# Cross-attention on one core: two max-row transfers a slot instead of four, and `wo` loaded ahead of slot 0

## The reference, cut to what matters

```python
Q = (query @ w_q.T).reshape(B, S, 16, 32).transpose(0, 2, 1, 3)
K = (key @ w_k.T).reshape(B, -1, 16, 32).transpose(0, 2, 1, 3)
V = (value @ w_v.T).reshape(B, -1, 16, 32).transpose(0, 2, 1, 3)
scores = jnp.einsum('bhqd,bhkd->bhqk', Q, K) / np.sqrt(32)
attn = jax.nn.softmax(scores, axis=-1)
ctx = jnp.einsum('bhqk,bhkd->bhqd', attn, V).transpose(0, 2, 1, 3).reshape(B, S, 512)
x = ctx @ w_o.T + b_o + query
mu = jnp.mean(x, axis=-1, keepdims=True)
var = jnp.mean(jnp.square(x - mu), axis=-1, keepdims=True)
return (x - mu) * jax.lax.rsqrt(var + 1e-5) * ln_gamma + ln_beta
```

## Time and profile before

| | |
|---|---|
| median of 3 executions | 559.01 us (558.89 to 560.57) |
| profiled execution, its time | 557.26 us |
| its span | 555.5 us |
| TensorE (PE) matmul busy | 532.4 us, 96% |
| VectorE (DVE) busy | 465.2 us, 84% |
| GpSimd (POOL) busy | 424.2 us, 76% |
| ScalarE (ACT) busy | 393.6 us, 71% |

### The profile page before, as it was taken

One profiled execution on the slowest core, in us unless ns is written; L12 is line 12 of the kernel. 1 busy time (PEld: TensorE's weight loads), 2 busy tenths in 40 slices (PEclk: granted clock), 3 DMA queues, 4 the chain that ended last, 5 costly groups with the idle time before them and its releaser, 6 DMA issues.

```text
span 555.5 us, 12699 instructions
## 1 busy us (share of the span) xinstructions
PE 532.4 (96%) x4522; PEld 363.1 (65%) x4522; DVE 465.2 (84%) x874; ACT 393.6 (71%) x733; POOL 424.2 (76%) x391
## 2 busy tenths in 40 slices
PE   8988899999999999999999999999999999998991
PEld 6755566766676666666676667666676667665561
DVE  7877668888888888988889888988888888988785
ACT  7636767777777777777777777777777777766662
POOL 1714678888888888888888888888888888776665
PEclk9999999999999999999999999999999999999997
DMA  8434552443344334443343334343343432222122
GB/s 312 143 86 122 153 167 70 131 130 95 95 131 131 102 93 125 131 122 88 110 133 108 112 105 127 107 128 100 118 114 106 133 102 84 86 67 69 48 76 95
DMA packets 74111, 63.23 MB, mean 114 GB/s; under 512 B 46528, under 2 KB 46528, under 8 KB 74048
## 3 DMA queue, kind: packets, MB, share of 16 engines
q1 hardware_dynamic: 74048, 62.42, 37.0%
HBM read 39.58 MB, written 16.78 MB: 101 GB/s over the span
## 4 chain that ended last, share of the span: by engine, by line
PE 84%; DVE 5%; SPq 3%; DMA 3%; POOL 2%; issue 2%; ACT 1%; POOLq 0%; DVEq 0%; ACTq 0%
PE ps_q L410 45%; PE ps_o L416 12%; PE ps_c L372 10%; PE ps_s L345 7%; PE ps_s L355 3%; PE ps_q L283 2%; PE ps_s L283 2%; PE ps_o L283 2%; SPq L217 2%; DMA wo_raw<-in_woT 2%; DMA max_rows<-max_turned 1%; DVE half_max L703 1%; POOL y L879 1%; PE ps_c L290 1%; POOL y L877 1%
## 5 line engine op out<-in xcount | busy, mean ns | idle before, releaser
L410 PE MATMUL ps_q<-x_hi,wq_lo 64*128 64x512 f32 x448 | 185.8, 415 | 1.2 <-DVE values L668 1.1
L416 PE MATMUL ps_o<-wo_hi,c_lo 64*128 64x512 f32 x448 | 186.3, 416 | 0.0
L416 PE MATMUL ps_o<-wo_hi,c_hi 64*128 64x512 f32 x448 | 175.4, 392 | 0.0
L410 PE MATMUL ps_q<-x_hi,wq_hi 64*128 64x512 f32 x448 | 175.3, 391 | 0.0
L410 PE MATMUL ps_q<-x_lo,wq_hi 64*128 64x512 f32 x448 | 175.1, 391 | 0.0
L416 PE MATMUL ps_o<-wo_lo,c_hi 64*128 64x512 f32 x448 | 174.7, 390 | 0.0
L410 PEld LDWEIGHTS ps_q<-x_hi,wq_lo 64*128 64x128 f32 x448 | 82.5, 184 | 74.6 <-DVE z L747 44.4
L877 POOL TENSOR_TENSOR y<-y,gamma_row 128x512 f32<-128x512 f32 x60 | 77.8, 1296 | 58.4 <-ACT y L562 58.4
L849 POOL TENSOR_TENSOR x_lo<-xT_raw,x_hi 128x512 fp32r<-128x512 f32 x60 | 77.4, 1290 | 27.3 <-ACT x_hi L497 23.3
L855 POOL TENSOR_TENSOR c_lo<-c_raw,c_hi 128x512 fp32r<-128x512 f32 x64 | 82.9, 1295 | 16.7 <-ACT c_hi L497 16.7
L410 PEld LDWEIGHTS ps_q<-x_hi,wq_hi 64*128 64x128 f32 x448 | 82.6, 184 | 16.2
(11 more groups left out here) (104 smaller groups left out, 1113.6 us busy)
## 6 DMA issues: line engine op xcount, KB each, us to landing
xT_raw<-in_xT SPq DMA_DIRECT2D x64, 256.0 KB, 3.2
x_raw<-in_x SPq DMA_DIRECT2D x64, 256.0 KB, 2.8
out<-y SPq DMA_DIRECT2D x64, 256.0 KB, 2.4
max_rows<-max_turned SPq DMA_DIRECT2D x256, 16.0 KB
ctx_raw<-in_ctxT SPq DMA_DIRECT2D x4, 256.0 KB, 4.7
wk_raw<-in_wkT SPq DMA_DIRECT2D x4, 256.0 KB, 4.8
wq_raw<-in_wqT SPq DMA_DIRECT2D x4, 256.0 KB, 5.8
wv_raw<-in_wvT SPq DMA_DIRECT2D x4, 256.0 KB, 6.6
```

The costliest lines, as they stand in the source:

```text
L410: return nc.tensor.matmul(ps_q[:, 0, :], w[l][half, k, dims], x_[r][half, qc % 2, k, :], start=(half is lower and k == 0 and step == 0), s ...
L416: return nc.tensor.matmul(ps_o[:, 0, :], cx[l][half, k, tile], wo[r][half, k, :], start=(half is upper and k == 0 and step == 0), stop=(ha ...
```

## The change

It does five things.

1. The low part of the maxima is no longer a third part of `max_hl` but is written into quadrants 1 and 3 of part 1, with two reductions of 32 partitions in place of one of 128. `max_turned` has 32 columns instead of 64, and `fill_max_rows` issues two transfers instead of four. The rows of `select` follow.
2. `wo` is loaded in four transfers, one for each quadrant of 32 partitions and all four slices. They are issued before slot 0, and behind them the bias row, gamma, beta and tiles 0 to 3 of x. Tiles 4 to 7 of x stay in slots 2 to 5, one in each.
3. In slots 1 to 3 `subtract_max(t - 1)` stands before `project_values`.
4. In slot 6 VectorE does `odd_values` before `turn_max`; for slot 61 it does `turn_max` before `divide` and `statistics`.
5. At the end ScalarE makes the shift of tiles 59, 60 and 61 itself, in two small activations, `invert_deviation(57)` moves ahead of `context_to_hi(62)`, and VectorE does `finish(58)` before `statistics(59)`.

```diff
-        max_hl, max_turned = sb("max_hl", [P, 3, 32], fp32r), sb("max_turned", [P, 2, 32], fp32)
+        max_hl, max_turned = sb("max_hl", [P, 2, 32], fp32r), sb("max_turned", [P, 32], fp32)
...
-                        row = 64 * pair + 8 * part + 4 * head + pair
+                        row = 64 * pair + 4 * head + 2 * part + pair
...
-                for pair in range(2):
-                    for part in range(2):
-                        row = 64 * pair + 8 * part
-                        sp.dma_start(max_rows[row:row + 8, n % 2, :].bitcast(fp32).rearrange("p (b j) -> p b j", j=32),
-                                     max_turned[:, part, :]).then_inc(max_rows_filled[n % 2], 16)
+                for row in (0, 64):
+                    sp.dma_start(max_rows[row:row + 8, n % 2, :].bitcast(fp32).rearrange("p (b j) -> p b j", j=32),
+                                 max_turned[:, :]).then_inc(max_rows_filled[n % 2], 16)
...
+            for quadrant, head in enumerate((0, 2, 1, 3)):
+                sp.dma_start(wo_raw[DK * quadrant:DK * (quadrant + 1), :, :],
+                             woT.rearrange("(k h d) n -> h d k n", k=KT, h=4)[head, :, :, :]).then_inc(wo_loaded, 16)
+            sp.dma_start(bias_row[:, :], b_o.partition_broadcast(P)).then_inc(bias_loaded, 16)
+            for row, src in ((gamma_row, gamma), (beta_row, beta)):
+                sp.dma_start(row[:, :], src.partition_broadcast(P)).then_inc(gains_loaded, 16)
+            for i in range(4):
+                load_x(i)
+            sp.wait_ge(keys_zeroed, 2)
+            sp.wait_ge(keys_lo_done, G)
             for t in range(OUT_LAG):
                 fill_max_rows(t)
                 load_ahead(t)
-
-                if 1 <= t <= KT:
-
-                    for head in range(2):
-                        sp.dma_start(wo_raw[64 * head:64 * (head + 1), t - 1, :],
-                                     woT_v[t - 1, :, :].rearrange("(p h d) n -> h p d n", p=2, h=2)[head, :, :, :]
-                                     ).then_inc(wo_loaded[t - 1], 16)
-                if t == 1:
-                    sp.dma_start(bias_row[:, :], b_o.partition_broadcast(P)).then_inc(bias_loaded, 16)
                 if 2 <= t <= 5:
-                    load_x(2 * t - 4)
-                    load_x(2 * t - 3)
-                if t == 5:
-                    for row, src in ((gamma_row, gamma), (beta_row, beta)):
-                        sp.dma_start(row[:, :], src.partition_broadcast(P)).then_inc(gains_loaded, 16)
+                    load_x(t + 2)
                 next_keys(t)
...
                 project_queries(t + 1)
+                if 1 <= t <= 3:
+                    subtract_max(t - 1)
...
-                if 1 <= t < OUT_LAG - 1:
+                if 3 < t < OUT_LAG - 1:
                     subtract_max(t - 1)
...
+            def shift_mean(i):
+                c = i % 8
+                nc.scalar.activation(shift[:, c:c + 1], mean_var[:, c, 0:1], ACT.Identity, scale=-1.0
+                                     ).then_inc(mean_negated_done, 1)
+                act.wait_ge(mean_negated_done, by_scalar(i) - by_scalar(59) + 1)
+                act.wait_ge(rstd_done, i + 1)
+                nc.scalar.activation(shift[:, c:c + 1], shift[:, c:c + 1], ACT.Identity, scale=rstd[:, c:c + 1]
+                                     ).then_inc(shift_done, 1)
...
-                nc.vector.tensor_reduce(max_hl[:, 2, :].bitcast(fp32),
-                                        max_hl[:, 0:2, :].bitcast(fp32).rearrange("p h b -> p b h"),
-                                        axis=AX.X, op=ALU.add).then_inc(max_lo_done, 1)
+                for first in (0, 64):
+                    nc.vector.tensor_reduce(max_hl[first + 32:first + 64, 1, :].bitcast(fp32),
+                                            max_hl[first:first + 32, :, :].bitcast(fp32).rearrange("p h b -> p b h"),
+                                            axis=AX.X, op=ALU.add).then_inc(max_lo_done, 1)
```

58 lines of the change are left out of this document (32 added, 26 removed).

## The result

The changed kernel takes **553.61 us** (median of 6, 552.40 to 555.06). The kernel before beside it took 558.95 (6 executions, 557.97 to 560.57); the ratio is 0.9899, 95% interval 0.9877 to 0.9921. It is faster by 5.3 us, and the forecast was 549.1 with a range to 552.6. The profiled execution took 552.51 us with a span of 550.5, against 557.26 and 555.5.

What follows compares the result with a forecast made beforehand. TensorE was taken to bound the loop (busy 436.47 of 436.98 us), leaving gains at the ends: 5.1 ahead, 0.5 in the loop, 4.3 last stage, sum 9.9; 559.0 - 9.9 = 549.1 us, own range 547.3 to 550.5, wider 547.0 to 552.6.

Steps and rivals of the forecast that it cites:

- Slots 4 and 5: Ahead of the loop: without waits for max rows both slots fall to 6.98 us, gaining 3.5 us together.
- The sentence on the outer dimension of 2: Loading of `wo`: the old source's outer dimension of 2 kept it on two transfer engines; the new one uses all.
- Slot 1: Ahead of the loop: the earlier subtraction lets value matmuls cover the exponential wait of 1.21 us, net gain 1.0 us.
- The rival of the front loads: Slot 1: front loads delay the first max rows, costing about 1 us; with GpSimd binding, 551.1 us; chance 0.14.
- Slot 6: Last slot ahead of the loop: VectorE's value copies and GpSimd's low parts both end near 68.3; gain 0.6 us.
- The loop: Main loop: the one stall of note, near 170 us, goes; gain 0.5 us, at most 0.8.
- Last stage: End of the program: removed VectorE waits and a shorter operation gain 4.3 us, bounds 2.4 and 5.2.
- the 0.85 for the earlier row of slot 61: Last stage: TensorE's 1.56 us wait for max rows goes; VectorE takes 1.0, less 0.15 for longer `turn_max`: 0.85 us.
- The 0.6 for the wait of tile 57: Last stage: VectorE's 1.12 us wait for `rstd` goes, but ScalarE's work for slot 63 moves back 0.5: 0.6 us.
- The 2.35 + 0.5 for tile 62: Last stage: the 2.66 us `rstd` wait shrinks by 2.35; the following 1.44 us operation sheds 0.5 of 0.7.
- rival on GpSimd's pace: Last stage: GpSimd ends last, six scaling operations taking 10.8 us instead of 8.7; 551.1 us; chance 0.12.
- The slower rival: Ahead of the loop: `wo` in bulk moves no faster, from 40 GB/s down, holding up ScalarE; 563 us; chance 0.04.

Runs made afterwards that it cites:

- e14: Kernel before, each slot's slice of `wo` loaded in four transfers of 32 partitions instead of two of 64, at the same place; 556.08 us, ratio 0.9951.
- e4: Changed kernel with only `wo` in front; bias, gamma, beta and x tiles issued behind the max rows, one or two a slot; 551.15 us, ratio 0.9864.
- e12: e4 with `subtract_max` of slots 1 to 3 put back behind `project_values`; 551.20 us, ratio 0.9865.
- e1: Kernel before with only the first part: low parts in the free quadrants, two max-row transfers a slot; 555.52 us, ratio 0.9949.
- e9: Changed kernel with `wo` still in front but in the old eight transfers of 64 partitions; 570.12 us, ratio 1.0201.
- e10: Changed kernel with bias, gamma and beta issued behind the max rows of slots 0 to 2; `wo` and x stay in front; 550.25 us, ratio 0.9848.
- e5: Changed kernel with GpSimd scaling by gamma and beta in only one column for tiles 56, 59, 60, 61; 549.54 us, ratio 0.9835.
- e6: Kernel before with GpSimd scaling by gamma and beta in only one column for tiles 56 and 59 to 61; 555.40 us, ratio 0.9929.

## Why the prediction was wrong

- **Slots 4 and 5** were right in size, 3.47 against 3.5, by a cause named too widely. I laid it to the traffic of these slots, eleven loads of it moved to the front; `wo`'s form alone is enough (e14). The sentence on the outer dimension of 2 was the right one, and the 9.00 us of the earlier trace rows its trace.
- **Slot 1**, 1.0: the step that failed is the rate. I took the front loads at 331 GB/s, the rate of the earlier trace rows. They moved at 226 to 257 until `wo` and the broadcast rows were through, so the queue was full until between 30 and 31 us, not 26.7. The margin of 0.55 us that I had worked out was spent, and slot 1 lost 0.18 instead of giving 1.0. The rival of the front loads is what happened, at its price of about 1 us. It named only `wo`, with its 32 partitions; the windows show `wo` slow (210 to 227 in e4), but the broadcast rows too (168 and 180). The mechanism of the gain was right (e4 and e12: 0.96).
- **Slot 6**, 0.6: 0.48. VectorE's copies still release the loop, as in the earlier trace rows, now with a wait of 0.61.
- **The loop**, 0.5: e1, e9 and e10, at 7.82 us a slot, took 430.3 against 431.0, so the stalls are worth 0.7 when they go. The profile shows +0.20, since the pace of 7.84 in this profile added 0.02 x 50 = 1.0. No row of one profile could show that.
- **Last stage**, 4.3: 1.70. Of the 0.85 for the earlier row of slot 61, the first scores of slot 63 came 1.61 earlier (5.45 to 3.84), but VectorE had only 0.5 of it at the division of slot 62, ahead of which it now waited 1.26 for ScalarE's `inverse` (0.48 before). The 0.6 for the wait of tile 57 came out as -0.23: the wait of 1.12 went, and the two operations grew from 1.76 to 2.76. The 2.35 + 0.5 for tile 62 gave 1.43. The step that failed is "I take 0.5 of the 0.7": it treats the long operations of the earlier trace rows as something to be shed, when removing the waits moves all of VectorE's finishing under GpSimd's scaling. e5 and e6 price it: 3.0 us after, 2.5 before. I had the 1.70 and 1.44 beside plain 0.75 before my eyes and a rival on GpSimd's pace, but charged it to GpSimd's end and not to VectorE, which ends last. The eight operations, which the forecast had 0.5 shorter, became 2.26 longer.
- **The slower rival** was the right mechanism for the old form, with its threshold set too low: it said 40 GB/s, where ScalarE would want `wo`. At 51 GB/s e9 was 16.5 us slower, since the first max rows stand behind `wo` in the queue and are wanted 13 us earlier than `wo` itself.
- **The signs that I named.** No wait for max rows in slots 4 and 5: right. SP's two issues near 1.4 us: right (1.50 and 1.35). No wait of ScalarE for `wo`: right. The matmul of slot 61's maximum without a wait: right. No wait for `rstd` of tile 62: right. Loop start near 68.3: missed, 69.91. A wait for max rows in slot 1 as a sign of the front loads: it came, 1.19. Slots longer than 7.82 as a sign that VectorE binds: misleading, as e1 shows.
- **The median** of three lay 1.75 above the profiled time; here it lies 1.10 above. This helped by 0.65, by luck and not by any step of the prediction.
